# Output rows added onto a DRAM copy of x by an accumulating transfer, and x for the statistics loaded 8 slots sooner, in a fused attention and mixture-of-experts kernel

## The chip, the cores and the metric

The kernel runs on one core of a Trainium2 chip. The metric is the device time of one execution in microseconds (us). The engines are PE (TensorE), DVE (VectorE), ACT (ScalarE), POOL (GpSimd) and SP (SyncE, which here only issues transfers); "SPq" in a row is SP's queue issuing.

## What is computed

x is [4, 2048, 256] in float32, that is T = 8192 rows of D = 256. Cut to what matters:

```python
def reference(x, norm_g, Wq, Wkv, Wout, out_norm_g, wr, w1, b1, w2, b2):
    xn = layernorm(x)
    s = attention(xn, ...)      # 8 heads of 64, one k and v for all heads, 2048 keys; @ Wout, layer norm
    g = silu(moe(xn, ...))      # 8 experts, top 2, capacity 2560 rows each
    return x + s * g
```

So each output row is x plus a product that is known only at the very end.

## The kernel before

The rows are cut into 64 tiles of 128 rows (`t_id`), four tiles to a group (`g`, 0 to 15), four groups to a batch entry. Every engine walks one common list of slots. In an attention slot, one step of scores (PE, L641), one exponential (ACT, L870), one split into a high and a low half (DVE, L1224) and one step of weighing (PE, L669 and L680, five steps behind) are done. A group takes 64 steps, and `base[g]` is its first slot. The list is: 42 starting slots; the first attention, groups 0 to 7 (516 steps); the experts (40 blocks of 8 slots "hidden" and 4 "second"); the second attention, groups 8 to 15 (516 steps); 48 closing slots.

All other work hangs on this list as side chains: generators that wait with `clock.at(slot)` and issue what falls to their engine. Each engine's queue is in order, so a wait holds up all that is behind it. In a slot the chains run in the order of the list given to `clock.run`. The chains that matter here:

- **statistics(g)**, for groups 4 to 15 every 24 slots of the first attention. SP loads 512 KB of x into the single buffer `s_xin` at slot S_AT - 4 (L1375) after `s_lo` of the group before (slot S_AT + 11 of that group); DVE takes bn_stats of it at S_AT (L940); the normalised rows are stored by SP at S_AT + 12 (L1378) and read back through four transposing transfers at S_AT + 15 (L1387).
- **prepare_kv(g)**, for groups from 4 on: SP transposes xn of group g into `xT` at KV_AT - 22, which is slot 16 of the group g - 4 (L1400, four transfers).
- **prepare_q**: for each tile one store of q (L1420) at slots 7, 23, 39 and 55 of a group, and eight transposes into `qT` (L1430) at slot 58.
- **project_out(t)**, one group later: ACT and DVE split the attention output into halves at O_SPLIT (L1155 on DVE, two buffers `o_hl` in turn), SP stores them at O_SPLIT + 2 (L1466), reads the group back through eight transposes (L1473) at O_TURN, PE multiplies at O_PROJECT (L618). In slots of the next group these are 11, 14, 17, 20 / 24 / 36, 44, 52, 60. Groups 7 and 15 (`BY_PE`) are transposed on PE instead.
- **combine(t)**, all 64 in the second attention and the closing slots, one about every 12 to 13 slots and in two interleaved series in part of it. POOL gathers the two expert rows by index (L1329, two transfers), ACT and DVE form the gated sum and its silu (L857, L1183, L861, L1187), DVE multiplies by the attention row (L1194) and adds x (L1199). SP loads the x tile (L1496) at C_AT and stores the result (L1499) at C_AT + 16.

POOL also computes an inverse root for every tile of q (L1273, 2 slots ahead of its use on DVE).

Of the kernel before, what the change touches and what calls it, by code (L numbers as in the profile page):

```python
# [69 lines left out]
def build_program(nc, x, norm_g, Wq, Wkv, Wout, out_norm_g, wr, w1, b1, w2, b2, out):  # L70
# [29 lines left out]
    x_rows = x.rearrange("b s d -> (b s) d")  # L100
    out_rows = out.rearrange("b s d -> (b s) d")
    x_groups = x_rows.rearrange("(g j p) d -> g p j d", j=GT, p=P)
    x_tiles = x_rows.rearrange("(t p) d -> t p d", p=P)
    out_tiles = out_rows.rearrange("(t p) d -> t p d", p=P)

    xn_rows = nc.dram_tensor("xn_rows", [T, 2 * D], F16).ap()
# [74 lines left out]
    for t in range(NT):  # L181
        g, j = divmod(t, GT)
        if g in BY_PE:
            at = experts_at + 4 * j if g == XG else place["post", 0, 0] + 1 + 6 * j
            O_SPLIT.append(at + 1)
            O_TURN.append(at + 4)
            O_PROJECT.append(at + 7)
        else:
            O_SPLIT.append(base[g + 1] + 11 + 3 * j)
            O_TURN.append(base[g + 1] + 24)  # L190
            O_PROJECT.append(base[g + 1] + 36 + 8 * j)
    C_AT = [base[XG + 1] + 20 + 13 * t if t < EARLY else O_SPLIT[t] + 8 if t // GT in BY_PE else
            base[t // GT + 1] + 34 + 12 * (t % GT) for t in range(NT)]
    C_ORDER = sorted(range(NT), key=lambda t: C_AT[t])
# [26 lines left out]
    with ExitStack() as ctx:  # L221
# [10 lines left out]
        def cut(row, i, shape):  # L232
            n = int(np.prod(shape))
            piece = row[:, i * n:(i + 1) * n]
            return piece if len(shape) == 1 else piece.rearrange("p (a b) -> p a b", a=shape[0])
# [81 lines left out]
        xgT = [cut(flat(att[(XG + 1) % 2], F16), i, [2 * DC, GP]) for i in range(2)]  # L317
        b2_rows = [cut(flat(vhl_row[1], F32), i, [D]) for i in range(2)]

        y_got = [cut(flat(w1_lo[0], F32), i, [TOP_K, D]) for i in range(2)]  # L320
        x_again = [cut(flat(w1_lo[1], F32), i, [D]) for i in range(2)]
        res = [cut(flat(w1_lo[1], F32), 2 + i, [D]) for i in range(2)]

        early_x = [cut(flat(att[g // 2], F32), g % 2, [GT, D]) for g in range(BG)]

# [16 lines left out]
        def work(buf, n):  # L342
# [52 lines left out]
        y_stored = [sem(f"y_stored{i}") for i in range(2)]  # L395
        c_loaded = [sem(f"c_loaded{i}") for i in range(2)]
        y_gathered = [sem(f"y_gathered{i}") for i in range(2)]
        x_again_loaded = [sem(f"x_again_loaded{i}") for i in range(2)]
        out_stored = [sem(f"out_stored{i}") for i in range(2)]
        f_first, f_both, c_tanh, c_silu, c_times, c_added = [sem(n) for n in (  # L400
            "f_first", "f_both", "c_tanh", "c_silu", "c_times", "c_added")]


        NPIECE = 3 + 4 * E
# [335 lines left out]
        def _(engine):  # L740
# [109 lines left out]
            def combine(t_id):  # L850
                i = C_SEQ[t_id]
                f, w = c_work[i % 2][:, 0:D], c_work[i % 2][:, D:2 * D]
                yield from clock.at(C_AT[t_id] + 8)
                act.wait_ge(y_gathered[i % 2], 16 * TOP_K * (i // 2 + 1))
                act.wait_ge(routed, N_ROUTE["all"])
                act.wait_ge(c_added, i - 1)
                nc.scalar.activation(f, y_got[i % 2][:, 0, :], ACT.Copy,  # L857
                                     scale=gate[0][:, t_id:t_id + 1]).then_inc(f_first, 1)
                yield from clock.at(C_AT[t_id] + 12)
                act.wait_ge(f_both, i + 1)  # L860
                nc.scalar.activation(w, f, ACT.Tanh, scale=0.5).then_inc(c_tanh, 1)  # L861
# [35 lines left out]
        def _(engine):  # L897
# [279 lines left out]
            def combine(t_id):  # L1177
                i = C_SEQ[t_id]
                f, w = c_work[i % 2][:, 0:D], c_work[i % 2][:, D:2 * D]
                s = c_rows[t_id % 2] if t_id < EARLY else s_rows[t_id % 3][:, :]  # L1180
                yield from clock.at(C_AT[t_id] + 10)
                dve.wait_ge(f_first, i + 1)
                nc.vector.scalar_tensor_tensor(out=f, in0=y_got[i % 2][:, 1, :], scalar=gate[1][:, t_id:t_id + 1],  # L1183
                                               in1=f, op0=ALU.mult, op1=ALU.add).then_inc(f_both, 1)
                yield from clock.at(C_AT[t_id] + 14)
                dve.wait_ge(c_tanh, i + 1)
                nc.vector.scalar_tensor_tensor(out=w, in0=w, scalar=1.0, in1=f, op0=ALU.add,  # L1187
                                               op1=ALU.mult).then_inc(c_silu, 1)
                if t_id < EARLY:
                    dve.wait_ge(c_loaded[t_id % 2], 16 * (t_id // 2 + 1))  # L1190
                dve.wait_ge(s_ready, t_id + 1)
                dve.wait_ge(o_rstd, t_id + 1)
                dve.wait_ge(c_silu, i + 1)
                nc.vector.scalar_tensor_tensor(out=w, in0=w, scalar=half_rstd[:, t_id:t_id + 1], in1=s, op0=ALU.mult,  # L1194
                                               op1=ALU.mult).then_inc(c_times, 1)
                dve.wait_ge(c_times, i + 1)
                dve.wait_ge(x_again_loaded[i % 2], 16 * (i // 2 + 1))
                dve.wait_ge(out_stored[i % 2], 16 * (i // 2))
                nc.vector.tensor_tensor(res[i % 2], w, x_again[i % 2], ALU.add).then_inc(c_added, 1)  # L1199

            def divide(hh):
                g, h = divmod(hh, H)
# [55 lines left out]
        def _(engine):  # L1258
# [61 lines left out]
            def combine(t_id):  # L1320
# [7 lines left out]
                for k in range(TOP_K):  # L1328
                    nc.gpsimd.indirect_dma_start(  # L1329
                        y_got[i % 2][:, k, :], None, expert_rows,  # L1330
                        bass.IndirectOffsetOnAxis(gather_from[k][:, t_id:t_id + 1], 0)).then_inc(y_gathered[i % 2], 16)

            def main(kind, a, b):
                pass

# [5 lines left out]
        def _(engine):  # L1341
# [25 lines left out]
            def statistics(g):  # L1367
                if 0 < g < BG:
                    yield from clock.at((0, 0, 1, 2)[g])
                    nc.sync.dma_start(early_x[g], x_groups[g]).then_inc(early_loaded[g], 16)  # L1370
                elif g >= BG:
                    yield from clock.at(S_AT[g] - 4)
                    if g > BG:
                        sp.wait_ge(s_lo, g)
                    nc.sync.dma_start(x_of(g)[:, :, :], x_groups[g]).then_inc(s_loaded, 16)  # L1375
# [14 lines left out]
            def prepare_kv(g):  # L1390
                b, gi = divmod(g, BG)
                if g < BG:
                    return
                yield from clock.at(KV_AT[g] - 22)
                sp.wait_ge(s_stored[g % 2], 16 * (g // 2 + 1))
                sp.wait_ge(q_projected, GT * (g - BG + 1))
                sp.wait_ge(kv_projected, g)
# [82 lines left out]
            def store_rows(fg):  # L1480
# [2 lines left out]
                nc.sync.dma_start(expert_groups[fg], yout[fg % 2]  # L1483
                                  ).then_inc(y_stored[fg % 2], 16)

            def combine(t_id):
                i = C_SEQ[t_id]
                yield from clock.at(C_AT[t_id])
                sp.wait_ge(expert_out, FG * GT)
                if t_id < EARLY:  # L1490
# [1 line left out]
                    if t_id >= 2:  # L1492
                        sp.wait_ge(c_times, C_SEQ[t_id - 2] + 1)
                    nc.sync.dma_start(c_rows[t_id % 2], attn_tiles[t_id]).then_inc(c_loaded[t_id % 2], 16)
                sp.wait_ge(c_added, i - 1)
                nc.sync.dma_start(x_again[i % 2], x_tiles[t_id]).then_inc(x_again_loaded[i % 2], 16)  # L1496
                yield from clock.at(C_AT[t_id] + 16)
                sp.wait_ge(c_added, i + 1)
                nc.sync.dma_start(out_tiles[t_id], res[i % 2]).then_inc(out_stored[i % 2], 16)  # L1499

            def main(kind, a, b):
                pass
# [2 lines left out]
                statistics(g) for g in range(NG)] + [bias(e) for e in range(E)] + [prepare_kv(g) for g in range(NG)] + [  # L1505
                prepare_q(t) for t in range(NT)] + [
                zero_rows(i) for i in range(NZERO)] + [move_rows(t) for t in range(NT)] + [load_routed(fg) for fg in range(FG)] + [project_out(t) for t in range(NT)] + [store_rows(fg) for fg in range(FG)] + [
                combine(t) for t in C_ORDER])
            for i in range(2):
                sp.wait_ge(out_stored[i], 16 * NT // 2)  # L1510
# [21 lines left out]
```

## Time and profile before

| what | us |
|---|---|
| median of three runs | 2841.09 |
| the three runs | 2839.52, 2841.09, 2857.08 |
| the profiled execution, as a run | 2839.19 |
| its span in the trace | 2837.4 |
| first attention, in the span | 65 to 1056 |
| experts | 1056 to 1910 |
| second attention | 1910 to about 2797 |

All stretches are in us from the span's start. An engine's busy time over the length of a stretch says how near it is to being the bound there; the idle time and what ended it says which wait is real. "PEclk" is the TensorE clock granted in the stretch, 1.00 being 2.4 GHz and 0.50 being 1.2 GHz.

### The profile page before, as it was taken

The page shows a single profiled execution, that of the slowest core. Times are in us where ns is not written, and L with a number is a line of the kernel's source. Part 1 is how long each engine was busy: PE and PEld are TensorE (multiplying, and loading weights), DVE is VectorE, ACT ScalarE, POOL GpSimd, SP SyncE. Part 2 cuts the span into 40 slices and gives each one's busy share as a digit, 9 for nine tenths or more (in the row PEclk, how much of TensorE's full clock was granted, in tenths as well). Part 3 has the DMA queues.
Part 4 walks back from the last instruction along what each step waited for, and adds up shares of the span by engine and source line. Part 5 has one row for each costly group of instructions (what it writes and reads, how often), then busy time and mean ns, then how long its engine had stood idle before and what let it go on. Part 6 is the DMA issues. An engine that isn't in the chain of part 4 may idle for free.

```text
span 2837.4 us, 136381 instructions
## 1 busy us (share of the span) xinstructions
PE 2603.0 (92%) x63045; PEld 1835.5 (65%) x63045; DVE 2040.7 (72%) x3077; ACT 1745.3 (62%) x2259; POOL 609.3 (21%) x428
## 2 busy tenths in 40 slices
PE   4988997988798999999999999999999999999996
PEld 3665665765566666666666666677666666666674
DVE  5887987989887874334334333338999999999986
ACT  6766766665665655445455554537767667777663
POOL 3111111210777510000000000002233333433302
PEclk8999998999999999999999999999999999999997
DMA  3354545331755522222313213112344434333321
GB/s 101 88 131 123 138 123 138 94 76 48 193 145 144 139 55 52 77 60 80 81 53 84 85 47 82 53 38 50 89 86 104 93 89 99 84 91 99 78 49 50
DMA packets 414316, 254.52 MB, mean 90 GB/s; under 512 B 292200, under 2 KB 378160, under 8 KB 413744
## 3 DMA queue, kind: packets, MB, share of 16 engines
q1 hardware_dynamic: 401456, 212.22, 29.8%
q0 software_dynamic: 12288, 33.57, 4.4%
q8 instruction: 494, 8.09, 1.2%
q14 instruction: 78, 0.64, 0.1%
HBM read 65.32 MB, written 113.25 MB: 63 GB/s over the span
## 4 chain that ended last, share of the span: by engine, by line
PE 56%; DVE 19%; issue 8%; SPq 6%; ACT 5%; DMA 4%; POOL 1%; DVEq 0%; POOLq 0%; ACTq 0%
PE bank L709 14%; PE pair L695 13%; PE pair L641 11%; DVE arena L1224 11%; PE bank L669 8%; PE bank L680 4%; PE bank L567 2%; ACT arena L870 2%; SPq L1430 2%; SPq L1387 2%; SPq L1473 2%; PE bank L618 2%; DMA s_xin<-in_L_attn_x 1%; DMA xn_rows<-s_hl 1%; ACT h_f L877 1%
## 5 line engine op out<-in xcount | busy, mean ns | idle before, releaser
L1224 DVE TENSOR_TENSOR arena<-arena 128x1024 bf16<-128x1024 f32 (+1 forms) x1032 | 1218.1, 1211 | 141.9 <-ACT arena L870 137.8
L870 ACT ACTIVATE arena<-pair 128x1024 f32<-128x1024 f32 (+1 forms) x1032 | 1040.1, 1017 | 381.6 <-PE pair L641 377.8
L669 PEld LDWEIGHTS bank<-vhl,arena 64*128 64x128 bf16 x32768 | 747.6, 95 | 272.8 <-issue 46.2
L641 PE MATMUL pair<-qT,kT 64*128 64x512 f16 x6144 | 862.6, 381 | 50.9 <-ACT arena L870 39.2
L669 PE MATMUL bank<-vhl,arena 64*128 64x64 bf16 (+1 forms) x32768 | 837.5, 191 | 28.4 <-issue 25.6
L680 PE MATMUL bank<-vhl,arena 64*128 64x65 bf16 x16384 | 610.6, 191 | 64.3 <-DVE arena L1224 46.7
L680 PEld LDWEIGHTS bank<-vhl,arena 64*128 64x128 bf16 x16384 | 408.1, 95 | 75.5 <-DVE arena L1224 50.4
L877 ACT ACTIVATE h_f<-pair,b1T 128x512 f32<-128x512 f32 x320 | 219.0, 684 | 379.8 <-PE pair L695 379.4
L1273 POOL TENSOR_TENSOR q_small<-q_small,minus_half 128x8 f32<-128x8 f32 x64 | 150.7, 2354 | 1403.2 <-DVE q_small L1128 1402.9
L709 PE MATMUL bank<-w_hl,arena 128*128 128x256 bf16 x3840 | 426.9, 273 | 0.4
L1230 DVE TENSOR_TENSOR arena<-h_f,arena 128x512 bf16<-128x512 f32 x320 | 221.5, 692 | 263.9 <-ACT arena L744 263.3
L709 PEld LDWEIGHTS bank<-w_hl,arena 128*128 128x128 bf16 x3840 | 375.2, 98 | 53.6 <-DVE att L1240 2.0
L641 PEld LDWEIGHTS pair<-qT,kT 64*128 64x128 f16 x6144 | 244.3, 94 | 229.1 <-issue 61.1
L695 PE MATMUL pair<-att,w_hi 128*128 128x512 f16 x1280 | 382.6, 381 | 1.8 <-DMA att<-routed_rows 1.8
L1240 DVE TENSOR_TENSOR att<-bank,vhl 128x256 f32<-128x256 f32 x160 | 67.9, 424 | 263.3 <-PE bank L709 261.8
L695 PE MATMUL pair<-att,w_lo 128*128 128x512 f16 x640 | 243.5, 381 | 0.0
L695 PEld LDWEIGHTS pair<-att,w_hi 128*128 128x128 bf16 x1280 | 125.4, 98 | 144.8 <-issue 2.2
L1329 POOL DMA_INDIRECT w_lo<-expert_rows,gather_from x128 | 182.8, 1428 | 117.2 <-DVE c_work L1183 90.2
L744 ACT ACTIVATE arena<-h_f 128x512 bf16<-128x512 f32 x320 | 201.4, 630 | 10.2
L1301 POOL DMA_INDIRECT routed_rows<-xT_out,scatter_to x128 | 166.1, 1298 | 86.9 <-issue 31.2
L1273 POOL TENSOR_TENSOR half_rstd<-o_small,minus_half 128x1 f32<-128x1 f32 x64 | 39.3, 614 | 399.7 <-DVE o_small L1166 399.4
L695 PEld LDWEIGHTS pair<-att,w_lo 128*128 128x128 bf16 x640 | 62.8, 98 | 76.1 <-issue 1.1
(190 smaller groups left out, 1536.3 us busy)
## 6 DMA issues: line engine op xcount, KB each, us to landing
routed_rows<-h_f SPq DMA_DIRECT2D x80, 256.0 KB, 4.0
expert_rows<-att SPq DMA_DIRECT2D x40, 512.0 KB, 2.8
raw<-in_L_ffn_w SPq DMA_DIRECT2D x32, 512.0 KB, 4.3
q_rows<-qhl SPq DMA_DIRECT2D x60, 256.0 KB
o_rows<-o_hl SPq DMA_DIRECT2D x56, 256.0 KB, 3.2
xn_rows<-s_hl SPq DMA_DIRECT2D x16, 512.0 KB, 3.0
xT_out<-xn_rows SPq DMA_DIRECT2D x64, 128.0 KB
w_lo<-in_L_attn_x SPq DMA_DIRECT2D x64, 128.0 KB
```

The source lines that it names most:

```text
L641: t = nc.tensor.matmul(into, kT[g // BG % 2][rows, k_part, keys], qT[g % 2][rows, h // 2 * 2 + q_part, :], start=(k_part + q_part == 0), s ...
L669: nc.tensor.matmul(bank[:, at:at + width], p_top[rows, s, cols, 1], V[rows, kb, of:of + width], start=(kb == 0 and qb == 0 and turn == 0 a ...
L680: t = nc.tensor.matmul(bank[:, at:at + DH + 1], p_lo[rows, s, cols], V[rows, kb, 0:DH + 1], start=False, stop=(kb == KB - 1 and turn == 1) ...
L695: t = nc.tensor.matmul(bank, w[e % 2][:, c, cols], xgT[fg % 2][:, kind, :], start=(n == 0), stop=(n == 3 * DC - 1))
L709: t = nc.tensor.matmul(bank[:, 0:D], h[fg % 2][:, f, cols], w2_hl[e % 2][:, f, at:at + D], start=(f == 0 and h is h_hi and at == 0), stop= ...
L744: return nc.scalar.activation(o, i, ACT.Copy)
L870: nc.scalar.activation(p_f32[:, n % NP, columns(n)], pairs[n % 2][:, columns(n)], ACT.Exp).then_inc(exped, 1)
L877: nc.scalar.activation(h_f32[k % 2], lent[k % 4], ACT.Gelu_apprx_tanh, bias=b1T[:, e * FC + f:e * FC + f + 1]).then_inc(gelued, 1)
L1224: nc.vector.tensor_tensor(p_lo[:, n % NP, c], p_f32[:, n % NP, c], p_top[:, n % NP, c, 1], ALU.subtract).then_inc(lowed, 1)
L1230: nc.vector.tensor_tensor(h_lo[fg % 2][:, f, :], h_f32[k % 2], h_hi[fg % 2][:, f, :], ALU.subtract).then_inc(h_rest, 1)
L1273: return nc.gpsimd.tensor_tensor(o, i, minus_half[:, 0:n], ALU.pow)
L1329: nc.gpsimd.indirect_dma_start(y_got[i % 2][:, k, :], None, expert_rows, bass.IndirectOffsetOnAxis(gather_from[k][:, t_id:t_id + 1], 0)).t ...
```

## The change

- The 128 KB loads of x for the combination (L1496) and the addition on DVE (L1199) are gone. Instead sixteen 512 KB transfers on SP (`copy_x`) copy x to the output inside DRAM, every 20 slots from 24 slots into the experts.
- The product is written to `res`, and POOL stores it with a transfer that adds to what is in DRAM, at C_AT + 15. It waits for all copies and for the product. SP no longer stores results.
- The wait of DVE for the store of two tiles before stands before the product.
- `s_xin` is loaded at S_AT - 12 for groups from 5 on, the transposes into `xT` are issued at KV_AT - 34 (slot 4 in place of 16).
- O_SPLIT is spaced by 4 in place of 3 (11, 15, 19, 23), O_TURN is 27 in place of 24, O_PROJECT 37 + 8j in place of 36 + 8j.

```diff
-            O_SPLIT.append(base[g + 1] + 11 + 3 * j)
-            O_TURN.append(base[g + 1] + 24)
-            O_PROJECT.append(base[g + 1] + 36 + 8 * j)
+            O_SPLIT.append(base[g + 1] + 11 + 4 * j)
+            O_TURN.append(base[g + 1] + 27)
+            O_PROJECT.append(base[g + 1] + 37 + 8 * j)
...
-                act.wait_ge(c_added, i - 1)
+                act.wait_ge(c_times, i - 1)
...
-                nc.vector.scalar_tensor_tensor(out=w, in0=w, scalar=half_rstd[:, t_id:t_id + 1], in1=s, op0=ALU.mult,
-                                               op1=ALU.mult).then_inc(c_times, 1)
-                dve.wait_ge(c_times, i + 1)
-                dve.wait_ge(x_again_loaded[i % 2], 16 * (i // 2 + 1))
                 dve.wait_ge(out_stored[i % 2], 16 * (i // 2))
-                nc.vector.tensor_tensor(res[i % 2], w, x_again[i % 2], ALU.add).then_inc(c_added, 1)
+                nc.vector.scalar_tensor_tensor(out=res[i % 2], in0=w, scalar=half_rstd[:, t_id:t_id + 1], in1=s,
+                                               op0=ALU.mult, op1=ALU.mult).then_inc(c_times, 1)
...
+                yield from clock.at(C_AT[t_id] + 15)
+                pool.wait_ge(x_copied, 16 * NG)
+                pool.wait_ge(c_times, i + 1)
+                nc.gpsimd.dma_start(out_tiles[t_id], res[i % 2], accum_op=ALU.add).then_inc(out_stored[i % 2], 16)
...
-                    yield from clock.at(S_AT[g] - 4)
+                    yield from clock.at(S_AT[g] - (12 if g > BG else 4))
...
-                yield from clock.at(KV_AT[g] - 22)
+                yield from clock.at(KV_AT[g] - (34 if g > BG else 22))
...
+            def copy_x(g):
+                yield from clock.at(experts_at + 24 + 20 * g)
+                nc.sync.dma_start(out_groups[g], x_copies[g]).then_inc(x_copied, 16)
...
-                sp.wait_ge(c_added, i - 1)
-                nc.sync.dma_start(x_again[i % 2], x_tiles[t_id]).then_inc(x_again_loaded[i % 2], 16)
-                yield from clock.at(C_AT[t_id] + 16)
-                sp.wait_ge(c_added, i + 1)
-                nc.sync.dma_start(out_tiles[t_id], res[i % 2]).then_inc(out_stored[i % 2], 16)
```

## Rows read from the trace of the kernel before

**Rows 1.** The page, part 1: busy time, share of the span, instructions.
```profile
PE 2603.0 (92%) x63045; PEld 1835.5 (65%) x63045; DVE 2040.7 (72%) x3077; ACT 1745.3 (62%) x2259; POOL 609.3 (21%) x428
```
**Rows 2.** Windows: length, busy us (instructions) per engine, PEclk, DMA share, GB/s.
```profile
65.00:1056.00 991.00, 875.19 (x28474) 625.87 (x28474) 832.27 (x1219) 637.71 (x744) 309.06 (x212) 0.96 0.47 116
1056.00:1910.00 854.00, 849.92 (x5944) 573.90 (x5945) 322.86 (x529) 433.24 (x672) 2.16 (x4) 1.00 0.25 66
1910.00:2100.00 190.00, 181.19 (x6094) 130.60 (x6093) 171.30 (x228) 138.11 (x166) 52.75 (x32) 0.99 0.29 71
2100.00:2700.00 600.00, 559.50 (x18908) 401.39 (x18901) 573.58 (x828) 423.31 (x525) 203.67 (x138) 1.00 0.39 92
```
**Rows 3.** Waits in 65 to 1056: total us, times, longest.
```profile
DVE bn_s L940 <- DMA s_xin<-in_L_attn_x: 27.3, 6, 8.8
ACT o_hl L744 <- DMA o_rows<-o_hl: 16.5, 3, 6.8
DVE q_n L1132 <- POOL q_small L1273: 10.0, 3, 4.7
DVE o_hl L1155 <- DMA o_rows<-o_hl: 9.7, 3, 4.7
PE bank L618 <- DMA att<-o_rows: 3.2, 1, 3.2
```
**Rows 4.** Timelines of SP, then DVE, 222 to 262: start, us, instructions [idle].
```profile
229.89 12.57 SPq L1473 DMA_TRANSPOSE att<-o_rows  x8
243.59 0.43 SPq L1375 DMA_DIRECT2D s_xin<-in_L_attn_x  x1
...
248.02 0.75 DVE L940 BATCH_NORM_STATS2 bn_s<-s_xin 128x6 f32<-128x256 f32 x2 [8.79 <-DMA s_xin<-in_L_attn_x]
```
**Rows 5.** Windows around the six waits for s_xin: the longest one, and the sum.
```profile
240.00:256.00 16.00, 7.91 (x192) 5.61 (x190) 7.84 (x19) 4.04 (x5) 5.08 (x2) 0.74 0.47 134
...
sum 105.00, PE 78.90 PEld 58.90 DVE 72.63 ACT 50.75 POOL 20.97; mean PE 13.15 PEld 9.82 DVE 12.11 ACT 8.46 POOL 3.49
```
**Rows 6.** Timelines of SP, then ACT, 460 to 482.
```profile
466.35 5.79 SPq L1400 DMA_TRANSPOSE xT<-xn_rows  x4
472.23 0.91 SPq L1466 DMA_DIRECT2D o_rows<-o_hl  x1
...
474.99 0.63 ACT L744 ACTIVATE o_hl<-att 128x512 bf16<-128x512 bf16 x1 [5.69 <-DMA o_rows<-o_hl]
```
**Rows 7.** Windows 460 to 482 and 840 to 858: their sum.
```profile
sum 40.00, PE 24.70 PEld 17.61 DVE 27.03 ACT 20.10 POOL 15.11; mean PE 12.35 PEld 8.81 DVE 13.51 ACT 10.05 POOL 7.55
```
**Rows 8.** Windows at the lower clock behind four of these stalls: one, and the sum.
```profile
247.50:257.80 10.30, 5.43 (x60) 3.26 (x62) 9.61 (x23) 0.65 (x2) 5.26 (x2) 0.50 0.24 92
...
sum 34.30, PE 18.22 PEld 11.48 DVE 27.03 ACT 9.56 POOL 14.05; mean PE 4.56 PEld 2.87 DVE 6.76 ACT 2.39 POOL 3.51
```
**Rows 9.** Groups by line, DVE, 2100 to 2700: count | busy us, mean ns | idle.
```profile
L1224 DVE TENSOR_TENSOR arena<-arena 128x1024 bf16<-128x1024 f32 x344 | 406.8, 1219 | 15.8 <-ACT arena L870 15.2 <-issue 0.3
L1199 DVE TENSOR_TENSOR w_lo<-c_work,w_lo 128x256 f32<-128x256 f32 x47 | 20.0, 425 | 1.6
```
**Rows 10.** Groups by line, POOL, 2100 to 2700, then 2800 to 2838.
```profile
L1329 POOL DMA_INDIRECT w_lo<-expert_rows,gather_from x94 | 137.7, 1465 | 107.3 <-DVE c_work L1183 88.2 <-issue 19.1
...
L1329 POOL DMA_INDIRECT w_lo<-expert_rows,gather_from x8 | 8.4, 1056 | 3.0 <-issue 1.6 <-DVE c_work L1183 1.4
```
**Rows 11.** Timelines of SP and PE near 2290; the chain from 612 to 623.
```profile
2285.63 12.25 SPq L1473 DMA_TRANSPOSE att<-o_rows  x8
2301.06 1.48 PE L618 MATMUL bank<-wo_hl,att 128*128 128x256 bf16 x12
...
615.46 3.49 DMA att<-o_rows
```
**Rows 12.** The last instructions: the chain, then the timelines of DVE and SP.
```profile
2828.67 3.47 DMA w_lo<-expert_rows,gather_from
...
2834.74 0.42 DVE L1199 TENSOR_TENSOR w_lo<-c_work,w_lo 128x256 f32<-128x256 f32 x1
...
2829.44 6.09 SPq L1499 DMA_DIRECT2D out<-w_lo  x3
```

More of the change, by code:

```diff
@@ L102, in build_program @@
     x_groups = x_rows.rearrange("(g j p) d -> g p j d", j=GT, p=P)
-    x_tiles = x_rows.rearrange("(t p) d -> t p d", p=P)
+    x_copies, out_groups = [rows.rearrange("(g n) d -> g n d", n=GP) for rows in (x_rows, out_rows)]
     out_tiles = out_rows.rearrange("(t p) d -> t p d", p=P)
@@ L318, in build_program @@
         b2_rows = [cut(flat(vhl_row[1], F32), i, [D]) for i in range(2)]
+        res = [cut(flat(w1_lo[1], F32), i, [D]) for i in range(2)]
         y_got = [cut(flat(w1_lo[0], F32), i, [TOP_K, D]) for i in range(2)]
-        x_again = [cut(flat(w1_lo[1], F32), i, [D]) for i in range(2)]
-        res = [cut(flat(w1_lo[1], F32), 2 + i, [D]) for i in range(2)]
         early_x = [cut(flat(att[g // 2], F32), g % 2, [GT, D]) for g in range(BG)]
@@ L397, in build_program @@
         y_gathered = [sem(f"y_gathered{i}") for i in range(2)]
-        x_again_loaded = [sem(f"x_again_loaded{i}") for i in range(2)]
+        x_copied = sem("x_copied")
         out_stored = [sem(f"out_stored{i}") for i in range(2)]
-        f_first, f_both, c_tanh, c_silu, c_times, c_added = [sem(n) for n in (
-            "f_first", "f_both", "c_tanh", "c_silu", "c_times", "c_added")]
+        f_first, f_both, c_tanh, c_silu, c_times = [sem(n) for n in (
+            "f_first", "f_both", "c_tanh", "c_silu", "c_times")]
         NPIECE = 3 + 4 * E
@@ L1484, in store_rows @@
                                   ).then_inc(y_stored[fg % 2], 16)
+            def copy_x(g):
+                yield from clock.at(experts_at + 24 + 20 * g)
+                nc.sync.dma_start(out_groups[g], x_copies[g]).then_inc(x_copied, 16)
             def combine(t_id):
-                i = C_SEQ[t_id]
                 yield from clock.at(C_AT[t_id])
@@ L1507, in _ @@
                 zero_rows(i) for i in range(NZERO)] + [move_rows(t) for t in range(NT)] + [load_routed(fg) for fg in range(FG)] + [project_out(t) for t in range(NT)] + [store_rows(fg) for fg in range(FG)] + [
+                copy_x(g) for g in range(NG)] + [
                 combine(t) for t in C_ORDER])
```

## The prediction

> **What bounds the kernel now.** I read the page first: PE is busy for 92% of the span and DVE for 72% [rows 1], which hides that the stages differ. So I cut the span into its stages with the windows view. In the experts PE is busy for 849.9 of 854 us: nothing beside it can be won there, and anything with DMA room is free, since the DMA share is 0.25 [rows 2]. In the first attention PE is idle for 991 - 875.2 = 115.8 us and DVE for 158.7: neither is full, so single waits set the time. From 2100 to 2700 DVE is busy for 573.6 of 600 us (95.6%) and PE for 559.5 (93.2%): DVE is the tighter one, PE close behind [rows 2].
>
> Next the list of waits of the first attention. DVE stood 27.3 us, in six waits, before bn_stats, for the x load. ACT stood 16.5 us and DVE 9.7 us for the store of an attention half to free its buffer [rows 3]. The timelines show why, and it is SP's queue both times. At 229.9 SP began eight transposes that held it for 12.6 us; the x load, due in their midst, went out at 243.6 and DVE waited 8.8 us [rows 4]. At 466.3 four transposes of xn held it for 5.8 us; the store of a half went out behind them at 472.2 and ACT waited 5.7 us [rows 6].
>
> **The change, part by part.** The sum is made against the profiled execution, 2839.2 us as a run; the median of the three runs is 1.9 us above it, which I add at the end.
>
> *x loaded 8 slots sooner.* The load now falls in the slot of the store of the group before, 12 slots ahead of bn_stats. A slot here is 991 / 516 = 1.92 us, so it has 23 us in place of 7.7; even behind a full set of eight transposes (12.6 us) and 4.4 us of flight (243.59 to 248.02 [rows 4]) it lands in time. One of the eleven moved loads (slot 59, behind the transposes of q at 58) has the least to spare, some 6 us. So the 27.3 us of DVE go. What is it worth to the end? In 105 us of windows around the six waits PE was idle for 26.1 us [rows 5]. Elsewhere in the first attention it is idle for (115.8 - 26.1 - 15.3) / (991 - 145) = 8.8% [rows 2, 5, 7], that is 9.2 us of 105: 16.9 us extra. Narrower windows would give less, since part of the loss is made up in the steps behind. I take 13.5; bounds 0 and 27.3.
>
> *xn transposed 12 slots sooner, splits spaced by 4.* The four transposes leave the slots where the halves are stored, and each half has 8 slots in place of 6 for its buffer. Two windows with such waits, 40 us, hold 15.3 us of PE idle [rows 7] against 8.8% of 40, 3.5: 11.8 extra. The later of them lies where SP also waits for scattered rows, which stays. I take 8; bounds 0 and 11.8. The third wait on DVE's side is in the same place.
>
> *The clock.* Behind four of these stalls PE was granted 0.50, that is 1.2 GHz: 34.3 us with 18.2 us of PE busy [rows 8]. It fell after PE had stood idle: in 240 to 256 it was busy for 7.9 of 16 us [rows 5]. At 2.4 GHz that work would take half, 9.1 us less; but DVE was busy for 27 of the 34 us, catching up. I take 5; bounds 0 and 9.1.
>
> *The addition on DVE.* 64 of 425 ns are gone, 27.2 us, 47 of them (20.0 us) from 2100 to 2700 [rows 9]. Only what DVE sets is won. Were it all, 27; but PE needs its 559.5 us, and in the lighter stretch before, with DVE at 90.2%, PE reached 95.4% [rows 2], at which 559.5 us take 586: 14 us. With DVE at 93% after the change PE will come to less than that. Some 12 of the 64 lie outside that stretch and give little. I take 12; bounds 0 and 27.2.
>
> *The projection one slot later, its transposes three.* The transposes start about two slots later against the PE work that needs them, 2 x 1.73 = 3.5 us. Before, from 2100 on, the last of eight had been issued 3.2 us ahead of PE in one group (2285.63 + 12.25 to 2301.06) [rows 11], 5 to 7.6 in others. It lands 3.5 us after its start, about 1.5 after its end [rows 11]. So most of 14 groups keep 0 to 4 us, a few fall short by 2 or 3. I take +3 net. Bounds: 0, and 14 x 3.3 = 46 if no group had slack.
>
> *The store on POOL.* A gather costs POOL 1.06 us alone and 1.47 beside a loaded DVE [rows 10]; I take 1.47 for the store, 64 x 1.47 = 94 us. POOL is busy for 204 of 600 us there [rows 2], so it fits: hidden by POOL's idle time, 0. The wait for the product is new in POOL's queue. Behind it stand the gathers (needed 8 slots after their own slot, so covered) and the roots of q, which DVE wants two slots later. POOL's wait ends when DVE passes the product, always a slot or more ahead of the q sum that the root waits for, or behind the root in the list; 1.47 us is under a slot. If the cover were gone, 28 roots late by up to 1.5 us, 42 us. The wait of DVE for the store of two tiles before has some 12 slots, 20 us, against 3.5 us for a gather [rows 12]: 0.
>
> The Trainium skill speaks against this placement: "SBUF — State Buffer", section "Who interferes with whom", says that GpSimd cannot write the descriptors of its transfers while DVE is in a two-port mode, and advises the SP queue instead. The same page gives about 3.1 us for such a transfer beside a DVE copy, against 0.62 alone; by that, as an estimate, 64 stores would cost POOL 198 us. The rows show 1.47 against 1.06 [rows 10], so the effect here is small, if it is that.
>
> *The copies.* Sixteen issues on SP in the experts, 0.43 us each like the x load [rows 4], beside a queue and DMA engines that are mostly free [rows 2]: 0. Gone from SP in the second attention are 128 short issues; nothing waited for them: 0.
>
> *The end.* Before, DVE finished at 2835.2, SP was done issuing at 2835.5, the span ended at 2837.4 [rows 12]. Now the product ends 0.5 us sooner, and POOL's transfer takes at least the 3.5 us that a gather takes from its start [rows 12], more for reading what it adds to. I take +2; bounds 0 and +5.
>
> Sum: -13.5 - 8 - 5 - 12 + 3 + 0 + 0 + 2 = -33.5. 2839.2 - 33.5 = 2805.7, and 1.9 for the median: 2808.
>
> **Rivals.**
> - *DVE's additions are worth their full length.* For it: DVE at 95.6%. Against it: PE at 93.2%, and the 14 us bound by PE's best share. 2808 - 15 = 2793. Chance 0.12.
> - *PE fills the second attention anyway.* PE and DVE alternate as the bound, the gain is lost in PE's order. 2808 + 12 = 2820. Chance 0.18.
> - *The stalls of the first attention only move.* SP's queue is as long as before; what stood behind the x load (transposes for the logits, q stores) becomes late in its place. Against it: they have 9 slots and more. 2808 + 26.5 = 2834. Chance 0.13.
> - *The other side: transposes of the attention output come too late.* One mechanism, at PE's L618, once a group. If each of 14 groups stands the full 3.3 us, 46 in place of 3: 2851. It turns the change into a loss from (33.5 + 3) / 14 = 2.6 us a group on. For it: a gap of 3.2 us against 3.5 taken away [rows 11]. Against it: the others had 5 and more, and DVE, lighter, will store its halves sooner. Chance 0.06.
> - *POOL's roots come late behind the stores.* The longest such wait before was 4.7 us, beside the scatters [rows 3]. 42 us on 28 roots: 2850. Chance 0.04. The page named above is the reason it stands here at all.
>
> **How the numbers follow.** The forecast has 0.47, with a range of its own of 2795 to 2822. The whole range, 2787 to 2846, takes in the full addition, the lost second stage and the moved stalls; below it lie only several upper bounds at once, above it the two late mechanisms. 1% is about what a measurement of this kernel can tell from no change, 28.4 us, so the limits are 2812.7 and 2869.5. Faster: 0.34 of the forecast's 0.47, all of the 0.12, 0.03 of the 0.18: 0.49. Slower than 2869.5 needs a late mechanism beyond its price together with a lost gain: 0.05. The rest, 0.46, is within.
>
> **What would show it.** Right: no DVE wait for s_xin beside a small first one; no wait of ACT for o_rows near 470; PE idle in the first attention near 90 us and PEclk at 0.97 or 0.98; from 2100 on DVE near 93% and PE near 94.5%; POOL about 90 us busier with no wait of DVE L1132 on it. Wrong: PE waiting for att<-o_rows in many groups; waits of DVE for out_stored or for POOL; a second attention as long as before with DVE idle; the experts above 854 us.

## The result and the profile after

The changed kernel takes 2863.97 us (median of 20 runs, 2855.5 to 2873.39) and the kernel before, on the same chips, 2848.41 us (20 runs, 2839.52 to 2859.6): a ratio of 1.0052, 95% interval 1.0038 to 1.0067. The forecast was 2808, with a range up to 2846. The change costs 0.5% where a gain of 1.2% was expected. Of the 56 us between 2808 and 2864, 7.3 lie in the kernel before: the forecast started from the median of three runs (2841.09), and 20 runs give 2848.41.

The page, part 1, of the kernel after (as [rows 1]):

```profile
PE 2607.0 (91%) x63045; PEld 1839.0 (64%) x63045; DVE 2015.9 (71%) x3013; ACT 1742.5 (61%) x2259; POOL 673.4 (24%) x492
```

DVE has 64 instructions and 24.8 us less, POOL 64 more, as the diff says. Yet the span is 2858.2 us against 2837.4. The windows by stage, after (columns as in [rows 2]):

```profile
65.00:1062.00 997.00, 876.92 (x28562) 629.21 (x28562) 833.63 (x1220) 635.71 (x743) 309.44 (x212) 0.97 0.47 116
1062.00:1916.00 854.00, 850.26 (x5867) 572.19 (x5868) 324.67 (x531) 435.46 (x675) 3.79 (x5) 1.00 0.28 76
1916.00:2100.00 184.00, 170.29 (x5794) 124.12 (x5793) 161.10 (x207) 128.22 (x153) 48.51 (x33) 0.99 0.30 63
2100.00:2700.00 600.00, 554.82 (x18482) 396.43 (x18480) 540.01 (x763) 415.72 (x520) 251.86 (x185) 0.98 0.40 79
```

From 2100 to 2700 DVE fell from 95.6% to 90.0%, but PE did not rise: it fell from 93.2% to 92.5%. Neither engine took the room that DVE was given. In the first attention PE is idle for 120.1 us, not the 90 that I expected (115.8 before). The experts are as before, with the sixteen copies in them. For stage lengths I take the time from the first to the last exponential of ScalarE in each attention. These are the rows of that line in the kernel after (ns of the shortest, median and longest, then first and last start in us):

```profile
L869 ACT ACTIVATE arena<-pair x516: 597/1024/1060, 67.2 to 1055.8; 128x1024 f32<-128x1024 f32 x169, 128x512 f32<-128x512 f32 x3
...
L869 ACT ACTIVATE arena<-pair x516: 592/1024/1052, 1912.4 to 2810.9; 128x1024 f32<-128x1024 f32 x169, 128x512 f32<-128x512 f32 x3
```

and of the kernel before:

```profile
L870 ACT ACTIVATE arena<-pair x516: 597/1025/1062, 68.9 to 1055.2; 128x1024 f32<-128x1024 f32 x169, 128x512 f32<-128x512 f32 x3
...
L870 ACT ACTIVATE arena<-pair x516: 592/1025/1048, 1911.1 to 2792.5; 128x1024 f32<-128x1024 f32 x169, 128x512 f32<-128x512 f32 x3
```

The first attention took 988.6 us against 986.3, although its largest stall is gone (without that stall and with nothing else changed it took 971.3, experiment e3 below); the second took 898.5 against 881.4. So some 17 us are lost in each of them. Waits of DVE, then of PE, in the first attention of the kernel after (as [rows 3]):

```profile
DVE arena L1220 <- ACT arena L869: 135.0, 115, 9.8
DVE q_n L1131 <- POOL q_small L1269: 9.4, 6, 3.8
DVE o_small L1159 <- PE bank L617: 6.1, 5, 2.9
...
PE bank L566 <- DVE s_rows L1173: 21.8, 9, 5.6
...
PE bank L617 <- DMA att<-o_rows: 8.6, 3, 5.9
PE bank L679 <- DVE arena L1220: 8.2, 13, 1.7
PE bank L534 <- DVE s_rows L1173: 4.7, 3, 2.0
```

The 27.3 us for s_xin are gone, and so are DVE's waits for o_rows. What has grown is a wait of PE's own: it waits before L566 (the product that gives q) and L534 (k and v) for **s_rows**, which neither of them reads (s_rows holds the projected rows, as DVE leaves them). The kernel before had this wait too, but smaller. Its rows, of the first attention and then of the second:

```profile
PE bank L680 <- DVE arena L1224: 27.9, 21, 6.5
PE bank L567 <- DVE s_rows L1174: 11.5, 8, 3.9
...
PE bank L535 <- DVE s_rows L1174: 2.6, 2, 1.7
...
PE bank L680 <- DVE arena L1224: 18.8, 25, 1.5
PE bank L567 <- DVE s_rows L1174: 4.0, 6, 1.3
PE bank L535 <- DVE s_rows L1174: 1.0, 2, 0.7
```

and in the second attention of the kernel after:

```profile
PE bank L566 <- DVE s_rows L1173: 17.0, 10, 2.7
...
PE bank L679 <- DVE arena L1220: 6.3, 16, 1.1
PE bank L534 <- DVE s_rows L1173: 4.1, 3, 2.3
```

Together these waits are 19.1 us before and 47.6 us after. The reason is in the code: all of PE's side products (the logits, k and v, q, the projection) take turns in **one** bank of PSUM, where the kernel has PE write its products. `side.take` hands over the bank, names the semaphore count at which its new content will have been read, and returns the count that the product before left. Cut from the code, the last four lines from `project_out`:

```
side_banks = [banks[3][:, :]]
...
bank, free = side.take(s_ready, t_id + 1)
where["o", t_id] = bank
if free:
    pe.wait_ge(*free)
```

The projection's turn ends with `s_ready`, when DVE has read its result through four instructions and written s_rows. One such turn in the kernel after, PE's timeline (start, us, instructions, idle before):

```profile
2328.85 1.48 PE L617 MATMUL bank<-wo_hl,att 128*128 128x256 bf16 x12
2330.27 0.82 PE L640 MATMUL pair<-qT,kT 64*128 64x512 f16 x6
...
2334.22 0.81 PE L566 MATMUL bank<-wq_hi,xT 128*128 128x512 bf16 x2 [2.39 <-DVE s_rows L1173]
2334.82 1.06 PE L566 MATMUL bank<-wq_lo,xT 128*128 128x512 bf16 x2
```

and DVE's:

```profile
2331.80 1.22 DVE L1220 TENSOR_TENSOR arena<-arena 128x1024 bf16<-128x1024 f32 x1
2332.94 0.42 DVE L1159 BATCH_NORM_STATS2 o_small<-bank 128x6 f32<-128x256 f32 x1
...
2333.68 0.47 DVE L1173 SCALAR_TENSOR_TENSOR s_rows<-bank,o_small,out_g 128x256 f32<-128x256 f32 x1
```

The bank is taken at 2328.85 and free at 2334.15 (2333.68 + 0.47), 5.3 us later: the product itself takes 1.5, DVE comes to it 2.6 us after that, having other work of its queue to do first, and its chain takes 1.2. The hold spans three slots of 1.73 us. The q product came one slot after the projection and stood for 2.39 us; PE's queue is in order, so all its other work stood with it. A turn of the same kind in the kernel before, two slots apart, PE's timeline and then DVE's:

```profile
2315.84 1.48 PE L618 MATMUL bank<-wo_hl,att 128*128 128x256 bf16 x12
...
2320.95 0.60 PE L567 MATMUL bank<-wq_hi,xT 128*128 128x512 bf16 x2 [0.76 <-DVE s_rows L1174]
2321.40 0.59 PE L567 MATMUL bank<-wq_lo,xT 128*128 128x512 bf16 x2
...
2320.43 0.47 DVE L1174 SCALAR_TENSOR_TENSOR s_rows<-bank,o_small,out_g 128x256 f32<-128x256 f32 x1
```

The hold was 5.1 us and the wait 0.76: the rotation was already one slot too tight, and this could be read before the change. The plan of slots says where the products meet. Counted from a group's first slot, q's products stand at 14, 30, 46 and 62 and those for k and v at 38; the projections stood at 36, 44, 52, 60 and now stand at 37, 45, 53, 61. So three of the four, 36, 44 and 60, went from two slots ahead of the next user to one. I folded the starts of the exponentials of the second attention over its groups of 64 slots, four slots to a row (own working from the trace, us for four slots, mean over the groups behind the first):

| slots of the group | before | after | |
|---|---|---|---|
| 36 to 39 | 7.99 | 9.33 | projection 37, k and v 38 |
| 44 to 47 | 9.31 | 10.51 | projection 45, q 46 |
| 60 to 63 | 7.82 | 9.78 | projection 61, q 62 |
| 20 to 23 | 7.07 | 6.25 | none |
| 56 to 59 | 7.44 | 6.77 | none |
| all 64 | 110.9 | 113.1 | |

The loss is where the bank changes hands, 4.5 us in three places; 2.3 come back elsewhere (it may be that DVE has less to do there; the table doesn't show why); 2.2 a group remain, some 17 us over the eight groups of the stage, and the stage is 17.1 us longer.

### The profile page after: what moved, and what is told of

Its sections match the earlier page's. It is cut to its first block and busy times, and to the rows that moved or that the text cites. A ratio compares the mean times of both kernels' runs of the same rounds, so it can differ in the third digit from the quotient of the medians.

```text
span 2858.2 us, 136218 instructions
## 1 busy us (share of the span) xinstructions
PE 2607.0 (91%) x63045; PEld 1839.0 (64%) x63045; DVE 2015.9 (71%) x3013; ACT 1742.5 (61%) x2259; POOL 673.4 (24%) x492
## 5 line engine op out<-in xcount | busy, mean ns | idle before, releaser
L1269 POOL TENSOR_TENSOR q_small<-q_small,minus_half 128x8 f32<-128x8 f32 x64 | 144.6, 2260 | 1272.7 <-DVE q_small L1127 1272.3
L815 ACT ACTIVATE q_f<-bank,rstd 128x512 f32<-128x512 f32 x63 | 43.3, 688 | 129.9 <-PE bank L566 129.5
```

The source lines that it names most:

```text
L1269: return nc.gpsimd.tensor_tensor(o, i, minus_half[:, 0:n], ALU.pow)
```

## The experiments

Two theories stood at the start. **A, the bank:** projections one slot later cost more than the rest of the change wins. **B, another part:** the adding transfers on POOL, the copies, or the moved transposes cost it. Each ratio below is against the kernel before on the same chip, with its 95% interval. The experiments fell on four chips, where the kernel before took 2834 to 2917 us, so times of different groups are not compared, only ratios. Each trace is of one execution, so its waits have no interval.

### The projection's slot

The change of one number, in the kernel before (e1), and its reverse in the kernel after (e2).

```diff
-            O_PROJECT.append(base[g + 1] + 36 + 8 * j)
+            O_PROJECT.append(base[g + 1] + 37 + 8 * j)
```

> The kernel before with one edit: the projection at slots 37, 45, 53, 61 in place of 36, 44, 52, 60. Theory of the bank: PE's projection, its product for k and v (slot 38) and its products for q (slots 14, 30, 46, 62) take turns in one PSUM bank, and each must wait until the reader of the one before is done. With one slot in place of two between projection and product, PE stands before the product until DVE has passed the projected rows. In the changed kernel PE's waits for these rows rose from 5.0 to 21.1 us in the second attention and from 14.1 to 26.5 in the first. Here: the same waits rise to over 40 us together, and the time rises by 15 to 35 us, to 2863 to 2883. Rival, the adding store and the copies are what costs: this edit alone gives no loss, 2848 within 8.

> The changed kernel with the projection back at 36, 44, 52, 60, all else as changed. Theory of the bank: the waits for the projected rows fall back to about 20 us in all, and the time falls by 15 to 35 us, to 2829 to 2849, less what PE then waits for the transposes of the attention output, which start at slot 27: up to 10 us. Rival, the adding store and the copies cost: the time stays at 2864 within 8.

e1: **1.0172** (1.0148 to 1.0197), 2881.41 against 2833.82 us. e2: **0.9963** (0.9947 to 0.998), 2823.46 us. This one number alone costs 1.7%, 48 us, more than the 15 to 35 expected; without it the change is a small gain. PE's waits of e1, first and then second attention:

```profile
PE bank L567 <- DVE s_rows L1174: 22.9, 9, 5.6
PE bank L535 <- DVE s_rows L1174: 6.2, 6, 2.0
...
PE bank L567 <- DVE s_rows L1174: 21.8, 11, 2.8
PE bank L535 <- DVE s_rows L1174: 6.0, 3, 3.1
```

The waits for s_rows rose from 19.1 to 56.9 us, by 37.8, for a loss of 48. In e2 they are 17.1 us against 47.6 after, 30.5 less, for a gain of 0.9%, 25 us. Theory B falls as the cause of the loss: the adding stores, the copies and the moved transposes are all in e2, and e2 is no loss.

If the bank is the cause, more distance must win. In the kernel before at 35 + 8j (e12), three slots ahead, and at 40 + 8j (e8), behind k and v's product and q's; in the kernel after at 40 + 8j (e7).

> The kernel before with the projection at 35, 43, 51, 59 and nothing else. Theory of the bank: one slot more between projection and product takes PE's waits for the projected rows from 18.5 us to under 8 and the time to 0.993 to 0.998. Rival, only the slot 61 and 45 are bad and three slots are no better than two: 0.998 to 1.002.

> The kernel before with the projection at 40, 48, 56, 64 and nothing else. Theory of the bank: its waits for the projected rows (18.5 us) fall under 5 us, time 0.994 to 0.998 of before. Rival, any later projection costs, as 37 did (1.0172), because what follows it is late: over 1.01.

> The changed kernel with the projection at 40, 48, 56, 64: two slots behind the products for kv (38) and q (46, 62) in place of one slot ahead, and 13 slots behind the transposes. Theory of the bank: PE's waits for the projected rows (48 us in the changed kernel) fall under 10 us, those for the transposes (10.6 us there, 22.3 with the projection at 36) go to 0, and the time is 0.985 to 0.992 of before. Rival, the wait only changes sides (the projection waits for ACT to read the bank after q): 0.995 or more.

e12: 0.9954 (0.9932 to 0.9976). PE's waits for s_rows, whole span:

```profile
PE bank L567 <- DVE s_rows L1174: 3.4, 2, 3.0
```

All but 3.4 of 19.1 us are gone and the time fell by 0.5%, 13 us: the mechanism works in both directions. But the bank has a user in front too. The projection now comes two slots behind the logits' product (35, 51 and 59 behind 33, 49 and 57) in place of three, and waited for DVE to read the logits, which cost 1.2 us in the kernel before:

```profile
PE bank L618 <- DVE logits L967: 15.0, 3, 12.2
```

The 12.2 us end at 255.4, and DVE itself had stood 10.7 us until 249.8 for s_xin: a stall of the reader passes to PE through the bank. With x loaded sooner as well (e13 below) this wait is 5.3 us.

e8: 1.0019 (1.0006 to 1.0032), no gain, where 0.994 to 0.998 was expected. The wait had only gone to the next user, the logits' product:

```profile
PE bank L497 <- DVE s_rows L1174: 17.5, 4, 11.0
```

The logits stand at 25 + 24k slots, one slot behind a projection at 40, 48, 56 or 64, four times in all. The longest of the four, 11.0 us, again lies behind a stall of DVE for s_xin (8.8 us). e7: 0.9949 (0.9931 to 0.9968), with 7.9 us of the same wait and none for q, k and v; 0.985 to 0.992 was expected. It isn't better than e5 below (0.992), which has 20.6 us of waits for s_rows. Part of it is in the traces: where the experts begin, PE waited for the routed rows for 7.5 us in e7 and 7.4 in e8, against 2.1 in e5 and 1.8 in the kernel before. Why the later projection delays them was not looked into.

Does only the distance count, or the place too? In e9 the projections and the q, k and v products were all set one slot later, in the kernel before. The loads, stores and transposes of q, k and v hang on the same numbers and move with them.

```diff
-    KV_AT += [base[g - BG] + 38 for g in range(BG, NG)]
+    KV_AT += [base[g - BG] + 39 for g in range(BG, NG)]
...
-        Q_AT.append(max(base[0] + 1, base[t // GT - 1] + 16 * (t % GT) - 2))
+        Q_AT.append(max(base[0] + 1, base[t // GT - 1] + 16 * (t % GT) - 1))
...
-            O_PROJECT.append(base[g + 1] + 36 + 8 * j)
+            O_PROJECT.append(base[g + 1] + 37 + 8 * j)
```

> The kernel before with the projection one slot later as in the first experiment (1.0172), and the products for kv and q one slot later as well (39; 15, 31, 47, 63), so that the two slots between them are there again. Theory of the bank: what counts is the distance, time back to 0.997 to 1.004 and the waits for the projected rows to 14 to 22 us. Rival, the slot itself counts (what else lies on DVE in 37, 45, 53, 61): 1.01 or more.

1.0063 (1.0039 to 1.0087), between what the bank alone (0.997 to 1.004) and the rival (1.01 or more) had said. With the distance restored, 1.7% became 0.6%: about two thirds of the loss is the distance, as PE's waits for s_rows, 30.8 us against 56.9 in e1 and 19.1 before, say too. The place counts for the rest, 18 us. In the trace 11.7 us more of waits for s_rows than before stand against it, and more waits of PE for q itself, whose transposes now end a slot later:

```profile
PE pair L641 <- DMA qT<-q_rows: 10.1, 8, 2.7
```

This was 3.4 us in one wait in the kernel before. The 11.7 and 6.7 us together are the size of the rest, in one execution. Why the s_rows waits didn't go all the way back isn't shown; it may be that DVE comes to s_rows later in the new slots.

### x for the statistics eight slots sooner

```diff
-                    yield from clock.at(S_AT[g] - 4)
+                    yield from clock.at(S_AT[g] - (12 if g > BG else 4))
```

> The kernel before with one edit: x for the statistics loaded 8 slots sooner. If the six waits of DVE for it (27.3 us) set the time as priced in the prediction (13.5 us and a part of the 5 for the clock), the first attention is 13 to 18 us shorter and the time 2830 to 2835. Rival, these stalls only move to the next one: DVE's wait for x is gone and the first attention is as long as before within 5 us, time 2843 to 2853.

**0.9942** (0.9923 to 0.9961): 16.4 us. DVE waits for s_xin no more. The window of the first attention:

```profile
65.00:1039.00 974.00, 869.20 (x28435) 624.77 (x28436) 832.74 (x1215) 636.21 (x742) 310.17 (x212) 0.98 0.49 118
```

PE is idle for 104.8 us there against 115.8, and the granted clock rose from 0.96 to 0.98; PE's work is 6.0 us shorter for it. The stage is 971.3 us, 15 less.

### The transposes of xn twelve slots sooner

Beside the line above, in the kernel before:

```diff
-                yield from clock.at(KV_AT[g] - 22)
+                yield from clock.at(KV_AT[g] - (34 if g > BG else 22))
```

> The kernel before with the x load 8 slots and the transposes of xn 12 slots sooner, nothing else. The x load alone gave 0.9942. If the waits for the buffers of the halves (ACT 16.5 us, DVE 9.7) were worth the 8 us of the prediction, now 0.991 to 0.992, and those waits are under 5 us. Rival, they were not on the path, or the transposes are in the way at their new slot: 0.994 or more.

0.994 (0.9919 to 0.9961), where e3 alone gave 0.9942. ACT and DVE no longer wait for o_rows, and no gain is seen. The two intervals leave some 8 us of room either way, so this pair alone doesn't exclude the 8 us of the prediction; e5 (0.992) against e3 and e4 together (0.993), and e10 (0.9915) against e14 (0.9904), differ by as little and in both directions. The chip of this run and of e10 to e12, and the one of e13 to e15, show waits that the profile labels "remote", here of ACT:

```profile
ACT arena L870 <- remote: 49.7, 14, 7.3
```

They are in every trace taken on these two chips. The ratios are against the kernel before on the same chip, so they are used, and the lengths of the stages are not.

### The addition, the adding store and the copies

e4 is the kernel after with all slots as before: only the copies in DRAM, the adding store and the missing addition are left. e11 is the kernel before without the load of x and the addition, stored by SP; its output lacks x.

```diff
-                dve.wait_ge(x_again_loaded[i % 2], 16 * (i // 2 + 1))
...
-                nc.vector.tensor_tensor(res[i % 2], w, x_again[i % 2], ALU.add).then_inc(c_added, 1)
+                nc.vector.scalar_tensor_tensor(out=res[i % 2], in0=w, scalar=half_rstd[:, t_id:t_id + 1], in1=s,
+                                               op0=ALU.mult, op1=ALU.mult).then_inc(c_times, 1)
```

> The kernel before with the copies, the adding store on POOL and without the addition on DVE, all slots as before. If DVE's 27 us of additions are worth 12, less 2 at the end: 2838, with the second attention 8 to 14 us shorter. Rival, PE fills it anyway: second attention within 4 us of before, time 2848 to 2852. Rival, the store on POOL costs: second attention longer, time over 2853, with waits of DVE for POOL.

> The kernel before without the addition of x and without its load: the product alone is stored, by SP as before. It leaves out the residual x, so it is the price of the 64 additions on DVE by themselves, with no copies and no store on POOL. If they are worth 12 us as in the prediction, 0.9958; and the adding store with its copies, which gave 0.9988 with the same DVE work taken away, costs the difference of 8 us. Rival, the additions are worth what that kernel gained, 3 us: 0.998 to 1.000, and the store and the copies cost nothing.

e4: 0.9988 (0.997 to 1.0006). e11: 0.9988 (0.9968 to 1.0008). The two agree: 64 additions less are worth some 3 us in place of 12, if anything, and copying and storing by POOL costs nothing beside that these runs can tell (to some 8 us). The profiled execution of e4 had a second attention of 869.6 us, 12 less than before, which would have looked like the forecast; its twelve timed runs did not. Against effects this small one execution is no measure.

### The transposes of the attention output, and the splits

e5 is the kernel after with all three O_ lists as before; e15 is the kernel before with the new O_SPLIT and O_TURN only.

```diff
-            O_SPLIT.append(base[g + 1] + 11 + 3 * j)
-            O_TURN.append(base[g + 1] + 24)
+            O_SPLIT.append(base[g + 1] + 11 + 4 * j)
+            O_TURN.append(base[g + 1] + 27)
```

> The changed kernel with splits, transposes and projection of the attention output at their old slots (11 + 3j, 24, 36 + 8j); the early loads, the early transposes of xn and the adding store stay. Alone, the early x gave 0.9942 and the adding store 0.9988 of the time before. If the early transposes of xn are worth the 8 us of the prediction: 0.990. If they are worth nothing: 0.993. PE's 22 us of waits for the transposes of the attention output, seen with the projection at 36 behind transposes at 27, go down to under 6 us. Rival, those waits are due to something else (the store, the early transposes): they stay, and the time stays at the 0.9963 of that run.

> The kernel before with the splits at 11 + 4j and the transposes of the attention output at 27, the projection left at 36. The transposes are then three slots later against PE: waits of PE for att<-o_rows of 15 to 25 us in 7 or more groups, time 1.003 to 1.006. Rival, the wider splits free the buffers sooner and make up for it: under 1.002.

e5: **0.992** (0.9903 to 0.9937), near what e3 and e4 give together (0.9942 x 0.9988 = 0.993). e2 differs from it only in these two lines and has 0.9963. Of PE's waits in e2 for the transposed output, first and second attention:

```profile
PE bank L617 <- DMA att<-o_rows: 13.8, 4, 6.1
...
PE bank L617 <- DMA att<-o_rows: 8.5, 5, 2.5
```

That is 22.3 us in nine waits against 4.7 in e5. It is the rival "transposes come too late" at half its price in waits (22.3 of 46 us) and a quarter of it in time (0.43%, 12 us), and it shows once the projection is back at 36; in the kernel after, with the projection a slot later, 10.6 us are left. But e15 gives 0.999 (0.997 to 1.0011), with 9.5 us of these waits, where 1.003 to 1.006 and 15 to 25 us were expected: in the kernel before the two lines cost nothing. Between nothing and 0.4% the price of this part stays open.

### Better versions

The cause found says how to do better: load x sooner, and set the projection a slot earlier.

```diff
-            O_PROJECT.append(base[g + 1] + 36 + 8 * j)
+            O_PROJECT.append(base[g + 1] + 35 + 8 * j)
...
-                    yield from clock.at(S_AT[g] - 4)
+                    yield from clock.at(S_AT[g] - (12 if g > BG else 4))
```

e13 is the kernel before with these two. e14 has the copies and the adding store beside them. e10 is e14 with the early transposes of xn too.

> The changed kernel with splits and transposes at their old slots (11 + 3j, 24) and the projection at 35, 43, 51, 59: three slots ahead of the products for kv (38) and q (46, 62). With the projection at 36 the same kernel gave 0.992. Theory of the bank: PE's waits for the projected rows, 20 us there, fall under 8 us, and the time is 0.985 to 0.990. Rival, the transposes come too late for the earlier projection: waits for att<-o_rows over 10 us, 0.992 or more.

> The kernel before with x for the statistics 8 slots sooner and the projection at 35 + 8j, nothing else. If the two gains add (0.9942 and 0.9954): 0.9896, within 0.987 to 0.992. Rival, they overlap (both fill the same gaps of PE): 0.993 or more.

> As the one before, with the copies and the adding store in place of the additions on DVE, xn transposed at the old slot. If all three gains add: 0.9885. If the early transposes of xn were what took something away in the kernel with all of it (0.9915), this one is at 0.990 or below; if the adding store does, it is slower than the one before by 0.002 or more.

e13: **0.990** (0.9868 to 0.9933), 2888.87 against 2917.43 us. e14: 0.9904 (0.9868 to 0.9941). e10: 0.9915 (0.9891 to 0.994), in another group of runs, where 0.985 to 0.990 was expected. PE's waits of e13 at the projection and at the products for q, k and v that were followed here, first attention; the second has none of them:

```profile
PE bank L618 <- DVE logits L967: 5.3, 4, 1.7
PE bank L567 <- DVE s_rows L1174: 2.9, 2, 2.5
...
PE bank L618 <- DMA att<-o_rows: 2.6, 1, 2.6
```

e13 beats the kernel before by 1.0% and, worked out from the two ratios (0.990 / 1.0052), the kernel after by 1.5%, and is two numbers away from the kernel before. What e3 and e12 give singly comes to 0.9942 x 0.9954 = 0.9896, as measured. The adding store and the early transposes add nothing to it that the intervals show.

## Why the prediction was wrong, point by point

| term of the sum | predicted, us | measured, us | from |
|---|---|---|---|
| x for the statistics, with the clock behind its stalls | -13.5 - 5 | -16.4 | e3 |
| xn transposed sooner, splits spaced | -8 | 0, within 8 | e6 against e3, for the transposes; the splits lie three rows below |
| addition on DVE | -12 | -3 | e4, e11 |
| projection one slot later | +3, with the next | +25 (+48 alone) | after against e2; e1 |
| its transposes three slots later (measured with the splits) | in the +3 | 0 to +12 | e15; e2 against e5 |
| store on POOL, copies | 0 | 0 | e4 against e11 |
| the end | +2 | +2.4, already in e4's -3 | traces |
| sum | -33.5 | +6 to +18 | ratio: +15 |

(A ratio is turned into us with the time of the kernel before on the same chip.)

*The step that failed is "The projection one slot later, its transposes three".* It took +3 us, and the projection's slot alone was worth +25 in this kernel. The step asked what comes late to the projection, and priced its transposes. It did not ask who comes behind it in the bank that it writes. The prediction names no PSUM bank at all, and its worst bound for this step, 46 us, was worked out from transposes; that e1's 48 us are close to it is chance. The rows were there: in the kernel before PE waited 19.1 us for s_rows at L567 and L535, more than for the outputs' transposes (3.2), which I took up [rows 3]. Rows 3 keep only the waits that the change seemed to touch. A wait whose releaser (s_rows) is no operand of the waiting product is the sign of a buffer that changes hands.

*x sooner* was right in mechanism and size: 18.5 us expected with the clock, 16.4 measured. *Its rival, that the stalls only move,* is refuted for this part by e3. The first attention came out as that rival says (988.6 us against 986.3), but what came in place of the stall has another cause.

*xn transposed sooner*: the mechanism was right, the waits for o_rows went. Its worth was taken from PE's idle time in two windows, 11.8 us beyond the average [rows 7]. That step failed too, as far as the intervals tell: no gain is seen from removing them. Why isn't shown; in the later window the scattered rows hold SP too, as I had noted, and PE's idle time there need not have been due to these waits.

*The addition*: mis-sized, 12 against 3. I took DVE at 95.6% to be the bound [rows 2]. (I also counted 12 of the 64 additions outside 2100 to 2700; with 47 inside [rows 9] it is 17.) The windows of e4 speak against it:

```profile
2100.00:2700.00 600.00, 566.07 (x19264) 409.07 (x19262) 562.33 (x789) 433.26 (x535) 258.34 (x183) 1.00 0.42 82
```

DVE is at 93.7% and PE at 94.3%, as forecast (93 and 94.5), in one execution; the twelve timed runs show 0.1%. The ring of scores, exponentials and products passes through all three engines, and a lighter DVE waited more for ACT's exponentials. DVE's splits from 2100 to 2700 (as [rows 9]), first in e4, then in the kernel after:

```profile
L1220 DVE TENSOR_TENSOR arena<-arena 128x1024 bf16<-128x1024 f32 x351 | 415.5, 1218 | 28.7 <-ACT arena L869 26.8 <-issue 1.6
...
L1220 DVE TENSOR_TENSOR arena<-arena 128x1024 bf16<-128x1024 f32 x333 | 395.7, 1218 | 50.2 <-ACT arena L869 50.1
```

It was idle for 15.8 us before these instructions in the kernel before [rows 9], for 28.7 in e4, where the additions are gone and all slots are as before, and for 50.2 after, while 333 were done in place of 344. PE standing for its bank gives late scores, late exponentials, and an idle DVE.

*POOL and the end* held. The store takes POOL 1.0 us, not the 1.47 of a gather, 63 us in all, not 94; no wait on POOL grew (DVE's for q_small 9.4 against 10.0 [rows 3]). From the last exponential to the end of the span it is 47.3 us against 44.9. The rival with POOL's roots has nothing for it. *The rival with the late transposes* has something: 22.3 us of waits in e2, at L617 as it said, though not enough to turn the change into a loss. The nine of them are 2.5 us on the mean, the "2 or 3" of the prediction, but nine are not "a few".

*What would show it*: no wait for s_xin, ACT's 5.7 us near 470 gone and a PEclk of 0.97 were seen; PE idle near 90 us (120.1), DVE near 93% and PE near 94.5% (90.0 and 92.5), and POOL 90 us busier (64) were not. "A second attention as long as before with DVE idle" stood under wrong, and it came, even longer.

## What to carry to other kernels

Before a product is moved in an in-order queue, list who writes the same buffer behind it, and set the slots between them against the time from the product to its last reader: here 5.1 to 5.3 us, three slots, where two were planned and one was left. A wait for something that the waiting instruction doesn't read is that list showing itself in the trace; take it up at whatever size, since one slot took 19 us of it to 57, and one slot the other way to 3. Count the wait of every user of the buffer, that of the moved one too: here it rose from 1 to 15 us with that last slot, until DVE's own stall was gone. An engine at 95% beside one at 93% is not a bound whose every saved microsecond counts: here 3 of 27 us did.

## What the runs showed of the hardware

- A transfer issued by POOL that adds to DRAM held its queue for 997 ns and landed 128 KB in 3.4 us from the issue; a gather from the same queue held it for 1509 ns. The group of lines, POOL, 2100 to 2700, after (as [rows 10]), and its issues:

```profile
L1325 POOL DMA_INDIRECT w_lo<-expert_rows,gather_from x94 | 141.8, 1509 | 71.8 <-DVE c_work L1182 49.3 <-issue 22.4
L1332 POOL DMA_DIRECT2D out<-w_lo x47 | 46.2, 997 | 99.4 <-DVE w_lo L1194 99.4
...
out<-w_lo POOLq DMA_DIRECT2D x47, 128.0 KB, 3.4
```

  DVE was busy for 90% of that stretch, and the last store, beside an idle DVE, took 0.85 us. The Trainium skill's "SBUF — State Buffer", section "Who interferes with whom", has the writing of descriptors blocked by DVE's two-port modes; here no run shows it. The same section says that tensor_tensor has no such mode, and 396 of DVE's 540 us are one: by that, the trace agrees.
- A short stall of PE came with a lower clock. Behind the 2.39 us above the q product took 1.06 us for two matmuls where it took 0.59 in the kernel before. Windows of the kernel after, before and behind that stall (columns as in [rows 2]):

```profile
2325.00:2334.00 9.00, 6.83 (x226) 5.14 (x222) 8.86 (x14) 4.90 (x7) 0.93 (x2) 1.00 0.12 34
2334.80:2338.00 3.20, 3.20 (x17) 0.97 (x17) 0.89 (x2) 1.23 (x3) 2.42 (x2) 0.52 0.48 132
```

  The granted clock fell from 1.00 to 0.52, from 2.4 to about 1.2 GHz, once PE had stood, and was 1.00 again from 2338 to 2342. From 2100 to 2700 it is 0.98 on the mean, where it was 1.00 [rows 2], 0.99 in e1 and 1.00 in e2, e4 and e5. Over the whole span it is 0.976 before and after: what the earlier x gave back of the clock in the first attention was lost again in the second, with the bank's stalls.
